# Five edits in the last stages of a four-layer convolution chain on one core: how the largest value is found, filling products, order of the first stacking, banks and split of the last convolution

## The chip, the cores and the metric

The kernel runs on one core of a Trainium2 chip. The metric is the device time of one execution in microseconds (us).

## What is computed

The input has 16 images of 32 channels, 28 by 28. Cut to its core, the reference is:

```
# layer 0: ternary weights, 32 -> 192 -> 192 -> 32 channels, plus the input
h = relu6(bn(conv1x1(x, ternarize(w1))));  h = relu6(bn(conv3x3(h, ternarize(w2))))
x = x + bn(conv1x1(h, ternarize(w3)))
# layer 1: two 3x3 convolutions of values rounded to 8 bits; the step is max(x)/255 over the WHOLE tensor
out = relu(bn(conv3x3(fake_quant_act(x), fake_quant_weight(w1))))
x = relu(bn(conv3x3(fake_quant_act(out), fake_quant_weight(w2))) + x)
# layers 2 and 3 (here "c" and "d"), each:
y = relu(bn(conv3x3(x, w) + b))
x = where(max|y| over the image of a channel < 0.001, 0, y)
```

## The kernel before

The 16 images are four chunks `c` of four images `g` (`NCH = 4`, `G = 4`); a chunk's four images of 32 channels fill the 128 partitions, 784 pixels in the free dimension. Every engine has its own instruction stream, written by hand, and waits on semaphores. The long first part (layer 0, one image after the other in `slot`) is untouched. The work around the change comes after it:

- **Projection of the last chunk.** `project(c, h, steps)` multiplies the output of layer 0's 3x3 convolution by `w3` for half `h` of the rows. Steps 0 and 1 read `h2a` (the first 128 hidden channels, as a high and a low part; semaphore `h2a_ready`), steps 2 and 3 read `h2b` (the other 64; `h2_ready`). Each step is four products of 128x392 into 32 output partitions each. VectorE (DVE) then adds the residual (`residual`, line 1026) and reduces each half to a maximum (line 1029). `keep_warm(n, bank)` (line 370) issues n products into a bank that nobody reads.
- **The global maximum.** `step(k)` on VectorE and `largest(n)` on TensorE (PE) find the largest value over all partitions, once ahead of each 8-bit convolution: a column maximum `mx` (line 1145), a transpose into one row (line 547), a reduction of that row (line 1147), a product with ones that copies the number to all partitions (line 549), the clamp at 1e-8 (line 1149), the reciprocal (line 1150).
- **The 8-bit convolutions.** `qconv` (line 559) is nine taps for each half chunk. VectorE scales (`ra`), ScalarE (ACT) rounds into `qi` (`quant`, line 774). ScalarE also rescales the residual `y0` of each chunk (line 799).
- **The tail.** A written list sets the order on all engines; "q" is the second 8-bit convolution, "c" and "d" are layers 2 and 3:

```
TAIL = [("q", 0), ("q", 1), ("q", 2), ("c", 0), ("q", 3), ("c", 1), ("d", 0), ("c", 2), ("d", 1),
        ("c", 3), ("d", 2), ("d", 3)]
```

For each chunk of "q" VectorE adds the residual into `t1` (in the array `va`, line 1249), and splits it into a high and a low half-precision part (`part`, lines 1253 and 1255). `stack(layer, c)` copies the parts into `kst` (in the array `big`): six pieces of 32x900 on VectorE (line 1224, or 1226 in layer d), two on ScalarE (line 813 or 815). The stacked 64 partitions are doubled to 128, by VectorE itself for four of the eight (layer, chunk) pairs (line 1232, semaphore `v_dup`), by a DMA on SP's queue for the others (line 289, `s_dup`). `lconv(layer, c)` (line 590) is 72 products of 32 columns of weights: two halves of nine taps of four products, one product for each image. `relu_l` (ScalarE, line 827) writes each half into `yb` (in the array `vh`). For "d" VectorE reduces both halves (line 1279), forms the mask `keep` (line 1281), and for the last chunk multiplies both halves by it (line 1285); SP then writes each half out (line 302).

Three waits of `lconv` matter: for the doubled stack, for the weights, and for the bank. Layer c uses PSUM banks 2 and 3, layer d banks 4 and 5 (`bank = 2 + 2 * layer`), so each convolution of a layer waits until ScalarE has read the one before it (`wait(pe, yb_ready, 2 * DONE_BEFORE[...])`).

Of the kernel before, what the change touches and what calls it, by code (L numbers as in the profile page):

```python
# [28 lines left out]
P = 128  # L29
B, C, H, W = 16, 32, 28, 28  # L30
HID = 192
G = P // C
# [47 lines left out]
PBANK = (0, 2, 3, 1)  # L80
QBANK = (0, 6)
LTAIL = [s for s in TAIL if s[0] != "q"]
DONE_BEFORE = {(k, c): (LTAIL.index((k, c - 1)) + 1 if c else 0) for k, c in LTAIL}

N1, N2, N3 = C * HID, HID * HID * TAPS, HID * C


def conv_seq(nc, x, params, w1, w2a, w2b, w3, wq1, wq2, wc, wd, out):
    with ExitStack() as ctx:
# [109 lines left out]
        keep_ready, last_ready = sem("keep_ready"), sem("last_ready")  # L199
# [50 lines left out]
        @block.sync  # L250
        def _(sp):
            for k in range(2):
                dy = slice(3 * HID * k, 3 * HID * k + 3 * HID)
                sp.dma_start(w2ar[:, dy], w2a[:, dy]).then_inc(s_w2a[k], 16)
            sp.dma_start(xin[:, 0, :], x[:, 0, :]).then_inc(s_x[0], 16)
            sp.dma_start(w2ar[:, 6 * HID:], w2a[:, 6 * HID:]).then_inc(s_w2a[2], 16)
            sp.dma_start(w3r[:, 0, :], w3[0:P]).then_inc(s_w3, 16)
            sp.dma_start(w3r[0:HB, 1, :], w3[P:HID]).then_inc(s_w3, 16)
            sp.dma_start(w3r[HB:P, 1, :], w3[P:HID]).then_inc(s_w3, 16)
            sp.dma_start(w2br[HB:P, :], w2b).then_inc(s_w2c, 16)  # L260
            for c in range(1, NCH):
# [12 lines left out]
            for g in range(G):  # L274
                q = slice(C * g, C * g + C)
                for k, w in enumerate((wq1, wq2)):
                    sp.dma_start(wqr[q, k, :], w).then_inc(s_wq, 16)
                for k, w in enumerate((wc, wd)):
                    sp.dma_start(wcr[q, k, :], w).then_inc(s_wc, 16)
            for c in range(1, NCH):  # L280
                spread(c)

            def dup(layer, c):

                if (layer, c) in V_DUP:
                    return
                sp.wait_ge(stack_v[layer], c + 1)
                sp.wait_ge(stack_a[layer], c + 1)
                sp.dma_start(kst[2 * C:P, layer, c % 2].rearrange("p g h w -> p (g h w)"),
                             kst[0:2 * C, layer, c % 2].rearrange("p g h w -> p (g h w)")).then_inc(s_dup[layer][c], 16)  # L290

            for kind, c in TAIL:
                if kind == "q":
                    dup(0, c)
                elif kind == "c":
                    dup(1, c)
                else:
                    pieces = 1 if c < NCH - 1 else 2
                    for h in range(pieces):
                        px = slice(HW // pieces * h, HW // pieces * (h + 1))  # L300
                        sp.wait_ge(*((o_ready, c + 1) if pieces == 1 else (last_ready, h + 1)))
                        sp.dma_start(out[:, c, px], om[:, c, px]).then_inc(s_out, 16)
            sp.wait_ge(s_out, 16 * (NCH + 1))

# [48 lines left out]
        def _(pe):  # L353
# [94 lines left out]
                                             skip_group_check=True)  # L448
                i.then_inc(convb_done, 1)

            def project(c, h, steps=(0, 1, 2, 3), bank=7):

                wait(pe, y0_ready, 2 * c + h if bank == 7 else 0)
                lower = slice(HB * h, HB * h + HB)
                for s in steps:
                    if s < 2:
                        pe.wait_ge((h2a_ready, h2_ready)[s], (c + 1) * G)
                    for g in range(G):
                        w, rhs = ((w3t[:, 0, :], h2a[:, g, s, HALF * h:HALF * h + HALF]) if s < 2 else
                                  (w3t[lower, 1, :], h2b[lower, g, s - 2, :]))  # L460
                        i = nc.tensor.matmul(ps[C * g:C * g + C, bank, :HALF], w, rhs, start=(s == 0), stop=(s == 3))  # L461
                if 3 in steps:
                    i.then_inc(proj_done, 1)
# [71 lines left out]
                slot(NCH - 1, g, last=True)  # L535

            pe.wait_ge(rb_ready, 2 * B)
            keep_warm(16, 6)
            project(NCH - 1, 0, (0,))
            project(NCH - 1, 1, (0,), bank=6)  # L540
            project(NCH - 1, 0, (1, 2, 3))
            project(NCH - 1, 1, (1, 2, 3), bank=6)

            def largest(n):

                pe.wait_ge(gm_go, 2 * n + 1)
# [28 lines left out]
            def lconv(layer, c):  # L575
# [9 lines left out]
                for h in range(2):  # L585
                    for t in range(TAPS):
                        dy, dx = divmod(t, 3)
                        r0 = HALF_ROWS * h + dy
                        for g in range(G):
                            i = nc.tensor.matmul(ps[C * g:C * g + C, bank + h, :HALF],  # L590
                                                 wst[:, layer, C * t:C * t + C],
                                                 kst[:, layer, c % 2, g, r0:r0 + HALF_ROWS, dx:dx + W],
                                                 start=(t == 0), stop=(t == TAPS - 1))
                    i.then_inc(lconv_done[layer], 1)

# [9 lines left out]
        def _(act):  # L605
# [187 lines left out]
                quant(c, 1)  # L793

            act.wait_ge(scale_ready, 2)
            for c in range(NCH):
                if c >= 2:
                    quant(c, 1)
                nc.scalar.activation(y0[:, c, :], y0[:, c, :], ACT.Identity, bias=col[:, SIG + 3:SIG + 4],
                                     scale=col[:, BD + 2:BD + 3]).then_inc(ys_ready, 1)  # L800

            def stack(layer, c):

# [14 lines left out]
            def relu_l(layer, c):  # L818
# [6 lines left out]
                for h in range(2):  # L825
                    act.wait_ge(lconv_done[layer], 2 * c + h + 1)
                    nc.scalar.activation(yb[:, n % 2, HALF * h:HALF * h + HALF], ps[:, 2 + 2 * layer + h, :HALF],  # L827
                                         ACT.Relu, bias=bn[:, BSH, k:k + 1],
                                         scale=col[:, SIG + 4 + layer:SIG + 5 + layer]).then_inc(yb_ready, 1)

            for kind, c in TAIL:
                if kind == "q":
                    stack(0, c)
                else:
                    relu_l("cd".index(kind), c)
                    if kind == "c":
                        stack(1, c)


        @block.vector  # L840
        def _(dve):
# [301 lines left out]
            def step(k):  # L1143
                dve.wait_ge(cmax_done, 2 * NCH * (k + 1))
                red(mx[:, 8:9], cm[:, k].rearrange("p c h -> p (c h)"), AX.X, ALU.max).then_inc(gm_go, 1)
                dve.wait_ge(gm_done, 2 * k + 1)
# [96 lines left out]
            for kind, c in TAIL:  # L1243
# [29 lines left out]
                else:  # L1273
                    at = LTAIL.index((kind, c))
                    m = keep[:, at:at + 1]
                    px = [slice(HALF * h, HALF * h + HALF) for h in range(2)]
# [4 lines left out]
                    ts(m, cm[:, 1, c, 0:1], cm[:, 1, c, 1:2], CUT, ALU.max, ALU.is_ge).then_inc(keep_ready, 1)  # L1281
                    if c == NCH - 1:
                        dve.wait_ge(keep_ready, at + 1)
                        for h in range(2):
                            ts(om[:, c, px[h]], yb[:, at % 2, px[h]], m, None, ALU.mult).then_inc(last_ready, 1)


# [45 lines left out]
```

## Time and profile before

| | us |
|---|---|
| median of 3 executions | 316.2 (316.17 to 317.35) |
| the profiled execution | 316.51 |
| its span, first to last instruction | 314.7 |
| TensorE busy in the span | 269.9 (86%) |
| VectorE busy | 260.5 (83%) |
| ScalarE busy | 183.4 (58%) |
| mean granted clock of TensorE | 0.988 of full speed |

The busy shares are averages over very different stages. From about 224 us on, which this change is about, the engines take turns; there the times at which an instruction starts, and what it waited for, tell more than shares do. All line numbers in rows are those of the kernel before.

### The profile page before, as it was taken

To read this page: it belongs to the slowest core of one execution; us is meant where nothing else is said; L and a number is where in the kernel's file an instruction comes from. 1 tells how busy PE (TensorE), PEld (TensorE's weight loads), DVE (VectorE), ACT (ScalarE), POOL (GpSimd) and SP (SyncE) were. 2 spreads that over 40 slices of the span, in tenths; PEclk is the share of its full clock that TensorE was granted. 3 is DMA by queue.
4 is the path that set the end of the run, shared out by engine and by line. 5 is a ranking of instruction groups with operands and counts; after the bars stand their busy time and mean duration, and the time that the engine had idled before them with its cause. 6 is when DMAs were issued, how large, how long until landed. Compare 5 with 4: busy or idle time off the path is not lost.

```text
span 314.7 us, 6016 instructions
## 1 busy us (share of the span) xinstructions
PE 269.9 (86%) x2341; PEld 149.8 (48%) x2341; DVE 260.5 (83%) x497; ACT 183.4 (58%) x262; POOL 13.1 (4%) x24
## 2 busy tenths in 40 slices
PE   1458898899999999999999999999989997474763
PEld 0223554455555555555555554555545454242432
DVE  6599989999999888898888897857377588999983
ACT  3686775856836756645575666583236393447541
POOL 4500000000000000000000000030000000000101
PEclk9999999999999999999999999999999999899979
DMA  7832002022100000000000000000000000502232
GB/s 213 228 79 53 2 1 72 15 68 53 27 2 0 2 0 3 0 0 0 0 0 0 0 2 1 2 0 2 0 2 0 0 2 1 118 3 61 70 95 102
DMA packets 5656, 10.07 MB, mean 32 GB/s; under 512 B 1729, under 2 KB 3969, under 8 KB 5633
## 3 DMA queue, kind: packets, MB, share of 16 engines
q1 hardware_dynamic: 5360, 9.27, 11.0%
q10 hardware_dynamic: 272, 0.49, 0.7%
q8 instruction: 15, 0.25, 0.3%
q14 instruction: 9, 0.07, 0.1%
HBM read 4.04 MB, written 1.61 MB: 18 GB/s over the span
## 4 chain that ended last, share of the span: by engine, by line
PE 58%; DVE 21%; ACT 8%; issue 6%; DMA 4%; POOL 1%; ACTq 0%; DVEq 0%
PE ps L421 13%; PE ps L417 8%; PE ps L407 8%; PE ps L446 7%; PE ps L442 5%; PE ps L559 4%; PE ps L431 4%; PE ps L384 3%; DMA par<-params_in 3%; DVE big L1226 2%; PE ps L590 2%; DVE va L967 2%; ACT big L813 2%; PE ps L461 2%; DVE vh L973 1%
## 5 line engine op out<-in xcount | busy, mean ns | idle before, releaser
L421 PE MATMUL ps<-hb,w2bt 128*128 128x392 f16 x288 | 55.0, 334 | 0.0
L590 PE MATMUL ps<-big,wst 128*32 128x392 f16 x576 | 28.6, 358 | 17.8 <-ACT vh L827 10.8
L669 ACT CAST vh<-va 128x1680 f16<-128x1680 f32 x16 | 25.5, 1592 | 30.3 <-PE ps L446 25.4
L417 PE MATMUL ps<-vh,w2at 128*128 128x392 f16 x192 | 37.9, 333 | 0.8 <-DVE ps L997 0.8
L421 PEld LDWEIGHTS ps<-hb,w2bt 128*128 128x128 f16 x288 | 27.7, 96 | 21.9
L407 PE MATMUL ps<-vh,wu 128*128 128x392 f16 x192 | 37.1, 345 | 1.0 <-DVE vh L973 1.0
L967 DVE TENSOR_TENSOR va<-hp 128x420 f32<-128x420 f32 x64 | 33.9, 592 | 0.5
L651 ACT ACTIVATE part<-ps,bn 128x392 f32<-128x392 f32 x32 | 21.7, 678 | 16.8 <-PE ps L384 16.7
L973 DVE TENSOR_TENSOR vh<-va,vh 128x1680 f16<-128x1680 f32 x16 | 30.5, 1908 | 0.5
L590 PEld LDWEIGHTS ps<-big,wst 128*32 128x32 f16 x576 | 16.6, 103 | 29.8 <-issue 14.9
L651 ACT ACTIVATE ra<-ps,bn 128x392 f32<-128x392 f32 x32 | 21.6, 676 | 13.6 <-PE ps L384 11.8
L446 PE MATMUL ps<-hb,w2bt 128*64 128x392 f16 x288 | 27.6, 334 | 0.0
L407 PEld LDWEIGHTS ps<-vh,wu 128*128 128x128 f16 x192 | 19.1, 100 | 16.2 <-issue 1.8
L384 PE MATMUL ps<-xk,w1t 96*128 (+1 forms) x60 | 20.6, 344 | 6.6 <-ACT part L651 5.7
L559 PE MATMUL ps<-qi,wqi 128*128 128x392 bf16 x144 | 25.0, 333 | 0.2
L417 PEld LDWEIGHTS ps<-vh,w2at 128*128 128x128 f16 x192 | 18.5, 97 | 14.0 <-DVE ps L997 1.1
L675 ACT ACTIVATE r2a<-ps,bn 128x784 f32<-128x784 f32 x16 | 16.0, 1000 | 12.5 <-DVE h2a L1013 6.0
L446 PEld LDWEIGHTS ps<-hb,w2bt 128*64 128x64 f16 x288 | 16.3, 108 | 8.6
L431 PE MATMUL ps<-vh,wu 128*64 128x392 f16 x96 | 19.4, 340 | 0.0
L431 PE MATMUL ps<-vh,wun 128*64 128x392 f16 x96 | 19.4, 339 | 0.0
L442 PE MATMUL ps<-vh,w2at 128*64 128x392 f16 x192 | 19.3, 337 | 0.0
L559 PEld LDWEIGHTS ps<-qi,wqi 128*128 128x128 bf16 x144 | 13.8, 97 | 11.3 <-ACT qi L774 1.0
(200 smaller groups left out, 409.8 us busy)
## 6 DMA issues: line engine op xcount, KB each, us to landing
xk<-xpart SPq DMA_DIRECT2D x45, 49.0 KB, 1.9
big<-big SPq DMA_DIRECT2D x4, 450.0 KB, 3.8
xin<-x_in SPq DMA_DIRECT2D x4, 392.0 KB, 8.5
y_out<-xin SPq DMA_DIRECT2D x3, 392.0 KB, 2.4
big<-w2a_in SPq DMA_DIRECT2D x3, 288.0 KB, 4.1
big<-w2b_in ACTq DMA_DIRECT2D x1, 432.0 KB, 6.4
big<-w2b_in SPq DMA_DIRECT2D x1, 432.0 KB, 8.2
y_out<-xin SPq DMA_DIRECT2D x2, 196.0 KB, 2.0
```

Of the source, the lines that this page charges most:

```text
L384: nc.tensor.matmul(ps[:, bank, :HALF], (w1t[:, 0:P], w1t[:, P:P + 2 * HB])[two], xk[:, j, HALF * h:HALF * h + HALF], start=True, stop=True ...
L407: i = nc.tensor.matmul(ps[:, PBANK[k], :HALF], weights(k, dx, False), vh[:, b, part, k, :, dx:dx + W], start=(part == 0 and dx == 0), stop ...
L417: nc.tensor.matmul(ps[:, PBANK[k], :HALF], weights(k, dx, False), vh[:, b, part, k, :, dx:dx + W], start=False, stop=False, skip_group_che ...
L421: i = nc.tensor.matmul(ps[:, PBANK[k], :HALF], w2bt[:, t, 0:P], rows(b, k // 3, t), start=False, stop=(t == TAPS - 1), skip_group_check=True)
L431: i = nc.tensor.matmul(ps[HB * q:HB * q + HB, 4, :HALF], weights(k, dx, True), vh[:, b, part, k, :, dx:dx + W], start=(part == 0 and dx == 0),
L442: nc.tensor.matmul(ps[HB * q:HB * q + HB, 5, :HALF], weights(k, dx, True), vh[:, b, part, k, :, dx:dx + W], start=False, stop=False, skip_ ...
L446: i = nc.tensor.matmul(ps[HB * q:HB * q + HB, 5, :HALF], w2bt[:, t, P:HID], rows(b, q, t), start=False, stop=(t == TAPS - 1), skip_group_c ...
L559: i = nc.tensor.matmul(ps[:, bank + h, :HALF], wqi[:, k, t, :], qi[:, c, r0:r0 + HALF_ROWS, dx:dx + W], start=(t == 0), stop=(t == TAPS - 1))
L590: i = nc.tensor.matmul(ps[C * g:C * g + C, bank + h, :HALF], wst[:, layer, C * t:C * t + C], kst[:, layer, c % 2, g, r0:r0 + HALF_ROWS, dx ...
L651: nc.scalar.activation(dst[:, HALF * h:HALF * h + HALF], ps[:, bank, :HALF], ACT.Relu, bias=bn[:, BSH, at:at + 1], scale=bn[:, BSC, at:at ...
L967: i = tt(va[:, k], d[x0], d[x1], op)
L973: tt(vh[:, b, 1].rearrange(v), va[:].rearrange(v), vh[:, b, 0].rearrange(v), ALU.subtract).then_inc(va_ready, 1)
```

## The change

1. **Partition maximum by one product.** `largest` is now one product: the column `mx` is repeated to 128 columns of weights (`mx[:, 8:9].to_broadcast([P, P])`), and the identity streams through, so that every partition receives the row of all 128 maxima. VectorE reduces that 128x128 result directly to a column, and clamps it.
2. **Fewer filling products.** Ahead of the last projection stood 16; now there are 3 ahead of it and 4 in its middle. Steps 0 and 1 of both halves go first and wait only for `h2a_ready`; steps 2 and 3 wait for `h2_ready`.
3. **First stack ahead of later rounding.** On ScalarE `stack(0, 0)` comes before the rounding and the rescaling of chunk 3.
4. **Last convolution in free banks.** ("d", 3) uses banks 0 and 1, and does not wait for `yb_ready`; instead it waits for `t1_ready` of chunk 2.
5. **Uneven halves.** ("d", 3) is split into 18 and 10 rows (504 and 280 pixels) instead of 14 and 14; the last multiplication by `keep` is shared: VectorE the first 392 pixels, ScalarE the last 392, each with a semaphore of its own.

```diff
+LBANK = {(k, c): 2 + 2 * "cd".index(k) for k, c in LTAIL}
+LBANK["d", NCH - 1] = 0
+DONE_BEFORE["d", NCH - 1] = 0
+LROWS = {(k, c): (HALF_ROWS, HALF_ROWS) for k, c in LTAIL}
+LROWS["d", NCH - 1] = (18, 10)
+def row_slices(k, c):
+    first = LROWS[k, c][0]
+    return slice(0, first), slice(first, H)
...
-                        sp.wait_ge(*((o_ready, c + 1) if pieces == 1 else (last_ready, h + 1)))
+                        sp.wait_ge(*((o_ready, c + 1) if pieces == 1 else (last_ready[h], 1)))
...
-                    if s < 2:
-                        pe.wait_ge((h2a_ready, h2_ready)[s], (c + 1) * G)
+                    if s in (0, late):
+                        pe.wait_ge(h2_ready if s else h2a_ready, (c + 1) * G)
...
-            keep_warm(16, 6)
-            project(NCH - 1, 0, (0,))
-            project(NCH - 1, 1, (0,), bank=6)
-            project(NCH - 1, 0, (1, 2, 3))
-            project(NCH - 1, 1, (1, 2, 3), bank=6)
+            keep_warm(3, 4)
+            project(NCH - 1, 0, (0, 1), late=2)
+            project(NCH - 1, 1, (0, 1), bank=6, late=2)
+            keep_warm(4, 4)
+            project(NCH - 1, 0, (2, 3), late=2)
+            project(NCH - 1, 1, (2, 3), bank=6, late=2)
...
-                nc.tensor.transpose(ps[0:1, 5, 0:P], mx[:, 8:9], ident[:]).then_inc(gm_done, 1)
-                pe.wait_ge(gm_go, 2 * n + 2)
-                nc.tensor.matmul(ps[:, 5, 0:1], ones[0:1, :], rowm[0:1, 0:1], start=True,
+                nc.tensor.matmul(ps[:, 5, 0:P], mx[:, 8:9].to_broadcast([P, P]), ident[:], start=True,
                                  stop=True).then_inc(gm_done, 1)
...
-                bank = 2 + 2 * layer
+                bank = LBANK["cd"[layer], c]
                 wait(pe, yb_ready, 2 * DONE_BEFORE["cd"[layer], c])
+                if ("cd"[layer], c) == ("d", NCH - 1):
+                    pe.wait_ge(t1_ready, NCH - 1)
...
             for kind, c in TAIL:
                 if kind == "q":
                     stack(0, c)
+                    if c == 0:
+                        quant(NCH - 1, 1)
+                        shifted(NCH - 1)
...
+            nc.scalar.mul(om[:, NCH - 1, HALF:HW], yb[:, at % 2, HALF:HW], keep[:, at:at + 1]).then_inc(last_ready[1], 1)
...
-                red(rowm[0:1, 0:1], ps[0:1, 5, 0:P], AX.X, ALU.max).then_inc(gm_go, 1)
-                dve.wait_ge(gm_done, 2 * k + 2)
-                link(ts(c1(GM + k), ps[:, 5, 0:1], 1e-8, None, ALU.max))
+                link(red(c1(GM + k), ps[:, 5, 0:P], AX.X, ALU.max))
+                link(ts(c1(GM + k), c1(GM + k), 1e-8, None, ALU.max))
```

The change moves instructions at three places. On TensorE, behind the last product of layer 0 (the `h2a` and `h2b` rows are the projection, w2at rows the fillers, `ident,mx` the maximum), stood:

```order
L370 MATMUL ps<-vh,w2at 128x392 x16
L461 MATMUL ps<-h2a,w3t 32x392 x12
L461 MATMUL ps<-h2b,w3t 32x392 x8
L461 MATMUL ps<-h2a,w3t 32x392 x4
L461 MATMUL ps<-h2b,w3t 32x392 x8
L370 MATMUL ps<-vh,w2at 128x392 x8
L547 MATMUL ps<-ident,mx 1x128
L549 MATMUL ps<-rowm,ones 128x1
```

and there stands now:

```order
L383 MATMUL ps<-vh,w2at 128x392 x3
L474 MATMUL ps<-h2a,w3t 32x392 x16
L383 MATMUL ps<-vh,w2at 128x392 x4
L474 MATMUL ps<-h2b,w3t 32x392 x16
L383 MATMUL ps<-vh,w2at 128x392 x8
L561 MATMUL ps<-ident,mx 128x128
```

All `h2a` products now stand ahead of all `h2b` products, with four fillers between them, and the maximum is one product of 128x128.

On ScalarE, ahead of and in the first stacks (`qi` is the rounding, `y` the rescaling, `big` the stacking), stood:

```order
L799 ACTIVATE y<-y,col 128x784 [waits scale_ready]
L799 ACTIVATE y<-y,col 128x784
L774 ACTIVATE qi<-ra,magic 128x15x28 [waits q_v]
L774 ACTIVATE qi<-ra,magic 128x13x28 [waits q_v]
L799 ACTIVATE y<-y,col 128x784
L774 ACTIVATE qi<-ra,magic 128x15x28 [waits q_v]
L774 ACTIVATE qi<-ra,magic 128x13x28 [waits q_v]
L799 ACTIVATE y<-y,col 128x784
L813 COPY big<-part 32x900 [waits part_ready0]
L813 COPY big<-part 32x900
```

and there stands now:

```order
L811 ACTIVATE y<-y,col 128x784 [waits scale_ready]
L811 ACTIVATE y<-y,col 128x784
L787 ACTIVATE qi<-ra,magic 128x15x28 [waits q_v]
L787 ACTIVATE qi<-ra,magic 128x13x28 [waits q_v]
L811 ACTIVATE y<-y,col 128x784
L830 COPY big<-part 32x900 [waits part_ready0]
L830 COPY big<-part 32x900
L787 ACTIVATE qi<-ra,magic 128x15x28 [waits q_v]
L787 ACTIVATE qi<-ra,magic 128x13x28 [waits q_v]
L811 ACTIVATE y<-y,col 128x784
```

The two stacking copies of chunk 0 moved ahead of three instructions of chunk 3.

On TensorE, the last three convolutions (("c", 3), ("d", 2), ("d", 3)) and their waits were:

```order
L590 MATMUL ps<-big,wst 32x392 [waits yb_ready,s_dup0_3]
L590 MATMUL ps<-big,wst 32x392 x71
L590 MATMUL ps<-big,wst 32x392 [waits yb_ready,s_dup1_2]
L590 MATMUL ps<-big,wst 32x392 x71
L590 MATMUL ps<-big,wst 32x392 [waits yb_ready,v_dup]
L590 MATMUL ps<-big,wst 32x392 x71
```

and are now:

```order
L603 MATMUL ps<-big,wst 32x392 [waits yb_ready,s_dup0_3]
L603 MATMUL ps<-big,wst 32x392 x71
L603 MATMUL ps<-big,wst 32x392 [waits yb_ready,s_dup1_2]
L603 MATMUL ps<-big,wst 32x392 x71
L603 MATMUL ps<-big,wst 32x504 [waits t1_ready,v_dup]
L603 MATMUL ps<-big,wst 32x504 x35
L603 MATMUL ps<-big,wst 32x280 x36
```

The last one has lost its wait for ScalarE's reads of the one before it, and has 36 wider and 36 narrower products.

## Rows read from the trace of the kernel before

**Rows 1.** Timeline from 216 us: start, length, engine, line, what, idle time before

```profile
224.38 2.83 PE L370 MATMUL ps<-vh,w2at 128*128 128x392 f16 x16
...
225.60 0.57 DVE L1019 SCALAR_TENSOR_TENSOR h2b<-r2b,h2b 128x392 f16<-128x392 f32 x1
227.13 0.68 PE L461 MATMUL ps<-h2a,w3t 128*32 128x392 f16 x12
...
227.75 0.51 PE L461 MATMUL ps<-h2b,w3t 64*32 64x392 f16 x8
...
228.31 0.62 DVE L1026 SCALAR_TENSOR_TENSOR y<-ps,bn,xin 128x392 f32<-128x392 f32 x1 [2.15 <-PE ps L461]
```

**Rows 2.** The same timeline, at the first global maximum

```profile
231.14 0.27 PE L547 MATMUL ps<-ident,mx 128*1 128x128 f32 x1 [0.72 <-DVE mx L1145]
231.45 0.28 DVE L1147 TENSOR_REDUCE rowm<-ps 1x1 f32<-1x128 f32 x1 [0.45 <-PE ps L547]
...
231.78 0.38 PE L549 MATMUL ps<-rowm,ones 1*128 1x1 f32 x2 [0.37 <-DVE rowm L1147]
...
232.19 0.16 DVE L1149 TENSOR_SCALAR col<-ps 128x1 f32<-128x1 f32 x1 [0.47 <-PE ps L549]
232.39 0.16 DVE L1150 RECIPROCAL col<-col 128x1 f32<-128x1 f32 x1
```

**Rows 3.** Timeline from 256 us, at the first stacks

```profile
255.79 4.40 PE L559 MATMUL ps<-qi,wqi 128*128 128x392 bf16 x25
255.79 0.98 DVE L1255 SCALAR_TENSOR_TENSOR part<-va,part 128x784 f16<-128x784 f32 x1
...
256.81 1.12 ACT L774 ACTIVATE qi<-ra,magic 128x420 bf16<-128x420 f32 x2
256.81 2.38 DVE L1224 COPY big<-part 32x900 f16<-32x900 f16 x6
257.83 1.03 ACT L799 ACTIVATE y<-y,col 128x784 f32<-128x784 f32 x1
258.77 1.88 ACT L813 COPY big<-part 32x900 f16<-32x900 f16 x2
260.74 1.09 DVE L1232 COPY big<-big 64x3600 f16<-64x3600 f16 x1 [1.55 <-ACT big L813]
...
261.98 3.24 PE L590 MATMUL ps<-big,wst 128*32 128x392 f16 x72 [1.79 <-DVE big L1232]
...
264.56 1.90 ACT L813 COPY big<-part 32x900 f16<-32x900 f16 x2 [3.92 <-DVE part L1255]
...
265.16 3.23 PE L559 MATMUL ps<-qi,wqi 128*128 128x392 bf16 x18
```

**Rows 4.** Chain of work that ended last, 296 to 315: start, length, what

```profile
305.73 0.69 ACT vh L827
...
306.55 3.27 PE ps L590 x70
...
309.84 0.69 ACT vh L827
...
310.55 0.57 DVE cm L1279
```

**Rows 5.** Timeline of the end

```profile
301.20 4.47 PE L590 MATMUL ps<-big,wst 128*32 128x392 f16 x72 [4.09 <-DMA big<-big]
...
303.99 1.09 DVE L1232 COPY big<-big 64x3600 f16<-64x3600 f16 x1
...
311.40 0.76 DVE L1285 TENSOR_SCALAR xin<-vh,keep 128x392 f32<-128x392 f32 x2
311.85 0.81 SPq L302 DMA_DIRECT2D y_out<-xin  x2
```

**Rows 6.** Busy time by stretch; third column from the end: PEclk

```profile
226.00:228.00 2.00, 2.00 (x28) 0.84 (x25) 0.17 (x1) 0.00 (x0) 0.00 (x0) 1.00 0.00 0
...
300.00:302.00 2.00, 0.80 (x12) 0.44 (x16) 1.85 (x4) 0.82 (x1) 0.00 (x0) 0.60 0.77 258
```

More of the change, by code:

```diff
@@ L198, in conv_seq @@
         v_dup = sem("v_dup")
-        keep_ready, last_ready = sem("keep_ready"), sem("last_ready")
+        keep_ready, last_ready = sem("keep_ready"), [sem(f"last_ready{h}") for h in range(2)]
         part_ready = [sem(f"part_ready{l}") for l in range(2)]
@@ L449, in pair_outer, with project @@
                 i.then_inc(convb_done, 1)
-            def project(c, h, steps=(0, 1, 2, 3), bank=7):
+            def project(c, h, steps=(0, 1, 2, 3), bank=7, late=1):
                 wait(pe, y0_ready, 2 * c + h if bank == 7 else 0)
@@ L537, in _ @@
             pe.wait_ge(rb_ready, 2 * B)
-            keep_warm(16, 6)
-            project(NCH - 1, 0, (0,))
-            project(NCH - 1, 1, (0,), bank=6)
-            project(NCH - 1, 0, (1, 2, 3))
-            project(NCH - 1, 1, (1, 2, 3), bank=6)
+            keep_warm(3, 4)
[4 more added lines that the diff above has]
+            project(NCH - 1, 1, (2, 3), bank=6, late=2)
             def largest(n):
-                pe.wait_ge(gm_go, 2 * n + 1)
-                nc.tensor.transpose(ps[0:1, 5, 0:P], mx[:, 8:9], ident[:]).then_inc(gm_done, 1)
-                pe.wait_ge(gm_go, 2 * n + 2)
-                nc.tensor.matmul(ps[:, 5, 0:1], ones[0:1, :], rowm[0:1, 0:1], start=True,
+                pe.wait_ge(gm_go, n + 1)
+                nc.tensor.matmul(ps[:, 5, 0:P], mx[:, 8:9].to_broadcast([P, P]), ident[:], start=True,
                                  stop=True).then_inc(gm_done, 1)
@@ L582, in lconv @@
                     pe.wait_ge(s_dup[layer][c], 16)
-                bank = 2 + 2 * layer
+                bank = LBANK["cd"[layer], c]
                 wait(pe, yb_ready, 2 * DONE_BEFORE["cd"[layer], c])
-                for h in range(2):
+                if ("cd"[layer], c) == ("d", NCH - 1):
+                    pe.wait_ge(t1_ready, NCH - 1)
+                for h, rows in enumerate(row_slices("cd"[layer], c)):
                     for t in range(TAPS):
                         dy, dx = divmod(t, 3)
-                        r0 = HALF_ROWS * h + dy
                         for g in range(G):
-                            i = nc.tensor.matmul(ps[C * g:C * g + C, bank + h, :HALF],
+                            i = nc.tensor.matmul(ps[C * g:C * g + C, bank + h, :W * (rows.stop - rows.start)],
                                                  wst[:, layer, C * t:C * t + C],
-                                                 kst[:, layer, c % 2, g, r0:r0 + HALF_ROWS, dx:dx + W],
+                                                 kst[:, layer, c % 2, g, dy + rows.start:dy + rows.stop, dx:dx + W],
                                                  start=(t == 0), stop=(t == TAPS - 1))
@@ L795, in _, with shifted @@
             act.wait_ge(scale_ready, 2)
-            for c in range(NCH):
-                if c >= 2:
-                    quant(c, 1)
+            def shifted(c):
                 nc.scalar.activation(y0[:, c, :], y0[:, c, :], ACT.Identity, bias=col[:, SIG + 3:SIG + 4],
                                      scale=col[:, BD + 2:BD + 3]).then_inc(ys_ready, 1)
+            for c in range(NCH - 1):
+                if c == 2:
+                    quant(c, 1)
+                shifted(c)
             def stack(layer, c):
@@ L824, in relu_l @@
                     act.wait_ge(*((part_ready[1], 2 * c2 + 2) if k2 == "c" else (o_ready, c2 + 1)))
-                for h in range(2):
+                for h, rows in enumerate(row_slices("cd"[layer], c)):
+                    px = slice(W * rows.start, W * rows.stop)
                     act.wait_ge(lconv_done[layer], 2 * c + h + 1)
-                    nc.scalar.activation(yb[:, n % 2, HALF * h:HALF * h + HALF], ps[:, 2 + 2 * layer + h, :HALF],
+                    nc.scalar.activation(yb[:, n % 2, px], ps[:, LBANK["cd"[layer], c] + h, :px.stop - px.start],
                                          ACT.Relu, bias=bn[:, BSH, k:k + 1],
@@ L837, in _ @@
                         stack(1, c)
+            at = LTAIL.index(("d", NCH - 1))
+            act.wait_ge(keep_ready, at + 1)
+            nc.scalar.mul(om[:, NCH - 1, HALF:HW], yb[:, at % 2, HALF:HW], keep[:, at:at + 1]).then_inc(last_ready[1], 1)
         @block.vector
@@ L1145, in step @@
                 red(mx[:, 8:9], cm[:, k].rearrange("p c h -> p (c h)"), AX.X, ALU.max).then_inc(gm_go, 1)
-                dve.wait_ge(gm_done, 2 * k + 1)
-                red(rowm[0:1, 0:1], ps[0:1, 5, 0:P], AX.X, ALU.max).then_inc(gm_go, 1)
-                dve.wait_ge(gm_done, 2 * k + 2)
-                link(ts(c1(GM + k), ps[:, 5, 0:1], 1e-8, None, ALU.max))
+                dve.wait_ge(gm_done, k + 1)
+                link(red(c1(GM + k), ps[:, 5, 0:P], AX.X, ALU.max))
+                link(ts(c1(GM + k), c1(GM + k), 1e-8, None, ALU.max))
                 link(nc.vector.reciprocal(c1(RS + k), c1(GM + k)))
@@ L1275, in _ @@
                     m = keep[:, at:at + 1]
-                    px = [slice(HALF * h, HALF * h + HALF) for h in range(2)]
+                    px = [slice(W * rows.start, W * rows.stop) for rows in row_slices(kind, c)]
                     for h in range(2):
@@ L1283, in _ @@
                         dve.wait_ge(keep_ready, at + 1)
-                        for h in range(2):
-                            ts(om[:, c, px[h]], yb[:, at % 2, px[h]], m, None, ALU.mult).then_inc(last_ready, 1)
+                        ts(om[:, c, 0:HALF], yb[:, at % 2, 0:HALF], m, None, ALU.mult).then_inc(last_ready[0], 1)
 def kernel(**inputs):
```

## The prediction, made before the changed kernel ran

> **What bounds the kernel now.** I read the chain that ended last first, then the timeline around each edit. From 224 us on no engine is the bound by itself; the chain hops between them, and what counts at each edit is which wait ends last.
>
> At 224.38 TensorE has finished layer 0, issues 16 fillers and reaches the first projection product only at 227.13; VectorE, whose residual needs both halves of the projection input, has had its last input (`h2b`) ready at 225.60 + 0.57 = 226.17 and then idles 2.15 us until 228.31 [rows 1]. The fillers are therefore on the path. Then comes the row of small steps of the global maximum: 231.14, 231.45, 231.78, 232.19, 232.39, each waiting for the one before [rows 2]; it occurs twice. At the first stack VectorE is ready at 256.81 + 2.38 = 259.19, but its doubling copy starts at 260.74, for ScalarE's two pieces ran from 258.77 only [rows 3]. From there to the last stack VectorE's own work sets the time, so a start that is earlier there moves everything behind it. At the end the last convolution starts at 306.55, behind ScalarE's read of the bank (305.73 + 0.69), and is followed by a read of 0.69 and a reduction of 0.57 [rows 4].
>
> **Edit 2, fewer fillers.** A filler takes (227.13 − 224.38) / 16 = 0.172 us. Three take 0.52: the `h2a` products start at 224.90. Three groups of four `h2a` products and the change of step behind them took 227.75 − 227.13 = 0.62, or 0.21 a group; the four groups now take 0.83, to 225.73. Four fillers, 0.69, to 226.42; with 0.1 for the change of tile, the `h2b` products start at about 226.5 instead of 227.75 [rows 1]. The gain is **1.25 us**. It can't exceed 227.75 − 226.2 = 1.55, since `h2b` isn't there before; with 0.2 us at each of three changes between fillers and products instead of 0.1 in all it would be 0.75. The eight fillers behind the projection and the maximum move with it, so no idle time of TensorE grows here. The granted clock is 1.00 in this stretch, that is 2.4 GHz [rows 6].
>
> **Edit 1, the maximum.** Before, from the transpose to the reciprocal: 232.39 − 231.14 = 1.25 us. Now: the product (M), the reduction of 128 columns (0.28 and 0.03 to the next; it read 128 elements of a partition before too) and a clamp (0.20, as between 232.19 and 232.39) [rows 2]. The gain is 1.25 − 0.51 − M = 0.74 − M. A product of this shape in single precision with 128 weight columns and 128 streaming columns isn't in the trace. Nearest rows: the product with ones is two passes with 128 weight columns and one streaming column, 232.19 − 231.78 = 0.41 to its reader; the transpose streams 128 columns once in 0.27, while 392 half-precision columns take 0.172 of issue, so 128 single-precision ones cost some 0.1. Two such streams, the first partly hidden behind the second weight load, make M = 0.41 + 0.10 to 0.20. I take 0.56: **0.18 us a time, 0.36 for both**. Bounds: M = 0.46 (one stream exposed by half) gives +0.28 a time, M = 0.85 (four streams exposed) gives −0.11.
>
> The rows show one record for the transpose and two for the product with ones [rows 2], and so two streams at least. A rule of the Trainium skill speaks against the edit: "TensorE: Matmul & The Clock Gate", section Terms, has transpose mode as four times faster for FP32 than an ordinary product. By that rule there are four streams, M is 0.41 + 0.3 = 0.71, and both steps together gain 0.06 us instead of 0.36; no run here yet shows which.
>
> The ten fillers behind the maximum (1.7 us) still fit ahead of the first rounded data. VectorE's order and waits stay, and TensorE waits once less.
>
> **Edit 3, the first stack.** ScalarE's three instructions of chunk 3 (256.81 to 258.86) now come behind its stack. The stack needs VectorE's parts, ready at 255.79 + 0.98 = 256.77, and can start at about 256.9 when the rescaling of chunk 2 has ended; it ends at 258.8, ahead of VectorE's own six pieces at 259.19. The doubling starts at 259.25 instead of 260.74: **1.49 us**. TensorE has its last product of chunk 2 at 260.19, so the convolution that waits for the doubling (261.98) can start at 260.5: little more than that was to be had [rows 3]. Cover for what is moved back: chunk 3's rounding, now ready at about 260.0, is first read by the products at 265.16 − 1.49 = 263.7 [rows 3]; its rescaled residual is read by VectorE only behind layer c's first stack. Both engines copying pieces at once costs nothing new: ScalarE's two took 1.90 at 264.56 beside VectorE's, and 1.88 at 258.77 mostly alone [rows 3]. If ScalarE's next stack (263.06 now) had to wait for chunk 3's work, it would lose; that ends at 260.9, 2.1 us ahead. Bounds 1.3 and 1.55.
>
> **Edit 4, free banks.** The doubled stack for the last convolution is ready at 303.99 + 1.09 = 305.08 [rows 5]. Convolution ("d", 2) ends at 301.20 + 4.47 = 305.67 [rows 5]; its last group of four started some 0.35 before and another can follow after 3.24 / 18 = 0.18 [rows 3], at 305.50. The last convolution now starts there and not at 306.55 [rows 4]: **1.05 us**. If a switch costs a full drain it starts at 305.70: 0.85. Convolution ("d", 2) took 4.47 here and 3.24 elsewhere [rows 3, 5], because the clock granted behind its 4.09 us wait was low (0.60 on average from 300 to 302 [rows 6], the lower level being 1.2 GHz); in an execution in which it is not, the new order can begin only at 305.1 (`v_dup`), which is 0.36 more, not 1.2. So 0.85 to 1.41.
>
> **Edit 5, uneven halves.** If time goes by columns, both halves together cost as before. ScalarE's read: 784 elements 1.03 [rows 3], 392 elements 0.69 [rows 4], so 280 elements 0.59: 0.10 less. VectorE's reduction: 0.57 for 392 [rows 4] and 0.28 for 128 [rows 2], so 280 take 0.45: 0.12 less. The first half's longer read and reduction (0.79 and 0.69, begun 1.0 us ahead of the second's products' end) stay hidden. The shared multiplication gains **nothing**: SP issues the two writes one after the other, 0.81 for both [rows 5], and the second can't be issued before about 0.4 behind the first whoever multiplies; ScalarE's piece would be ready at 0.65 behind `keep`, the write is issued at 0.85. Together **0.22 us**. Bound below: if four narrow products cost as much as four of 392 columns (0.18), the second half is 0.42 longer, and the edit loses 0.2.
>
> **The sum.** 1.25 + 0.36 + 1.49 + 1.05 + 0.22 = 4.37 us. From the profiled execution, 316.51 − 4.37 = 312.14 (its span 310.3 of 314.7). The median before is 0.31 lower, of three runs that spread over 1.2 us; I forecast **312.0 us**.
>
> **Rivals.**
> - *Four streams* (0.12). The product streams its 128 columns not twice but four times, three of them exposed: M = 0.41 + 0.3 = 0.71, 312.0 + 2 × 0.15 = 312.3. For it: single precision already costs 0.1 for 128 columns in one record, twice the half-precision rate. Against it: only two records. This is where the rule of the Trainium skill on transpose mode (above) would lead.
> - *A dear product* (0.05). The repeated column as weights or four passes make M over 0.9: the maximum loses 0.2 or more each time, 312.0 + 0.36 + 0.4 = 312.8. For it: no such form in the trace; against it: the product with ones takes 0.19 a record [rows 2].
> - *The narrow half isn't faster* (0.08). Issue, not columns, sets four narrow products: 312.0 + 0.42 = 312.4. For it: four products take 0.18 where one full one takes 0.172, so each start costs something. Against it: that is only 0.003 for each.
> - *The clock falls once more* (0.06). With 15 instead of 24 fillers a fall in the projection or the first 8-bit convolution doubles a product (0.172 to 0.33); ("d", 2) shows that a fall costs about 1.2 to 1.6 us: 313.6. Against it: TensorE was busy without a break here and still is.
> - *The start gained at the first stack is lost again* (0.04), because a DMA doubling or a rounding comes last further on: 313.5. Against it: the next read of what was moved is 3.7 us later.
> - *Slower than before* (0.02). One mechanism: the clock falls at the thinner projection and stays at 1.2 GHz through the 8-bit convolutions. Each product then costs 0.16 more; 28 products cancel the gain of 4.37, 38 make it slower by over 0.5%, all 144 give 335. Against it: the one low stretch here ended within 4 us of dense products.
>
> **How the numbers follow.** The forecast's own case has 0.63 and 311.0 to 312.9. The bounds of all edits together give a gain between 0.75 − 0.22 + 1.3 + 0.85 − 0.2 = 2.5 and 1.55 + 0.56 + 1.55 + 1.41 + 0.22 = 5.3, that is 311.2 to 314.0; it is unlikely that all lie at one end. With the offset of single runs I give **310.9 to 313.6**. A difference under 0.5% (1.6 us) can't be told from none: faster 0.95, same 0.03, slower 0.02.
>
> **What would show it.** In the changed profile: VectorE's first residual about 1.25 earlier and its wait well under 1 us; reciprocal 1.07 behind the start of the product (1.25 before); doubling copy of chunk 0 right behind VectorE's sixth piece, with no wait for ScalarE; the last two convolutions without a gap; the last reduction about 0.45 long; the two writes still 0.4 apart. The prediction is wrong if a PEclk under 1.00 appears between 224 and 260 us, if the product takes over 0.9 us to its reader, or if a wait of over 0.5 us appears that wasn't there.

## The result

The changed kernel takes **311.62 us** (median of 4 executions, 311.14 to 312.2) against 316.49 (316.17 to 317.35) before; the ratio is 0.9843, with a 95% interval of 0.9816 to 0.9870. The forecast was 312.0. In a later group of runs the ratio was 0.9866 (0.9842 to 0.9891), median 312.36.

The profiled execution took 312.2 us, with a span of 310.4 us and a mean clock of 0.970. Its timeline at the projection answers to [rows 1]:

```profile
223.46 0.67 PE L383 MATMUL ps<-vh,w2at 128*128 128x392 f16 x3
...
224.06 0.85 PE L474 MATMUL ps<-h2a,w3t 128*32 128x392 f16 x16
...
224.68 0.57 DVE L1043 SCALAR_TENSOR_TENSOR h2b<-r2b,h2b 128x392 f16<-128x392 f32 x1
...
224.84 0.84 PE L383 MATMUL ps<-vh,w2at 128*128 128x392 f16 x4
...
225.61 0.54 PE L474 MATMUL ps<-h2b,w3t 64*32 64x392 f16 x16
...
226.18 0.63 DVE L1050 SCALAR_TENSOR_TENSOR y<-ps,bn,xin 128x392 f32<-128x392 f32 x1 [0.93 <-PE ps L474]
```

From the first filler to VectorE's first residual 2.72 us pass, where it was 228.31 − 224.38 = 3.93; VectorE's idle time ahead of it fell from 2.15 to 0.93. TensorE's wait ahead of the maximum grew instead, from 0.72 to 1.43 (first row below); VectorE's chain sets the time there, and the granted clock stayed at 1.00. The same timeline at the first maximum, for [rows 2]:

```profile
229.01 0.46 PE L561 MATMUL ps<-ident,mx 128*128 128x128 f32 x2 [1.43 <-DVE mx L1169]
...
229.50 0.29 DVE L1171 TENSOR_REDUCE col<-ps 128x1 f32<-128x128 f32 x1 [0.64 <-PE ps L561]
229.83 0.15 DVE L1172 TENSOR_SCALAR col<-col 128x1 f32<-128x1 f32 x1
230.02 0.16 DVE L1173 RECIPROCAL col<-col 128x1 f32<-128x1 f32 x1
```

The product has two records and reaches its reader in 0.49 us (0.53 the second time); product to reciprocal is 1.01 and 1.04 where it was 1.25 twice. At the first stack, for [rows 3]:

```profile
254.23 1.89 ACT L830 COPY big<-part 32x900 f16<-32x900 f16 x2
254.23 2.38 DVE L1247 COPY big<-part 32x900 f16<-32x900 f16 x6
256.15 1.14 ACT L787 ACTIVATE qi<-ra,magic 128x420 bf16<-128x420 f32 x2
256.64 1.09 DVE L1255 COPY big<-big 64x3600 f16<-64x3600 f16 x1
```

Both engines copy side by side, and the doubling copy starts 0.03 us behind VectorE's pieces instead of 1.55. The end, for [rows 4, 5], in the chain and (two lines) the timeline:

```profile
293.21 3.84 DMA big<-big
297.06 0.04 issue
297.10 8.60 PE ps L603 x138
...
305.73 0.59 ACT vh L845
...
306.35 0.46 DVE cm L1302
...
307.07 0.62 ACT xin L861
```

```profile
307.07 0.42 DVE L1307 TENSOR_SCALAR xin<-vh,keep 128x392 f32<-128x392 f32 x1
307.53 0.33 SPq L315 DMA_DIRECT2D y_out<-xin  x1
```

The pause between the last two convolutions is gone, yet from the first product of ("d", 2) to the end of the last one of ("d", 3) the time is 8.57 us, and it was 8.59 (301.20 to 309.79). The windows of the same run show why:

```profile
294.00:296.00 2.00, 0.00 (x0) 0.00 (x0) 1.93 (x7) 0.93 (x2) 0.92 (x1) 0.76 0.85 180
296.00:298.00 2.00, 0.90 (x12) 0.46 (x16) 1.85 (x4) 0.92 (x1) 0.00 (x0) 0.50 0.74 251
298.00:300.00 2.00, 2.00 (x28) 0.97 (x24) 1.91 (x6) 1.17 (x2) 0.00 (x0) 0.50 0.04 8
300.00:302.00 2.00, 2.00 (x32) 1.04 (x28) 1.55 (x2) 0.69 (x1) 0.00 (x0) 0.53 0.00 0
302.00:304.00 2.00, 2.00 (x48) 1.01 (x44) 0.59 (x2) 0.68 (x1) 0.00 (x0) 1.00 0.00 0
```

The third column from the end is the granted clock. It was 0.50 (1.2 GHz) up to about 302, under some 4.8 us of dense products; before, under some 2.6 us of them (301.2 to 303.8).

The span's difference, 314.7 − 310.4 = 4.3, is then: projection 1.21, maximum 0.24 + 0.21, first stack 1.52, last two convolutions 0.02, end 0.18, and **0.92 that no edit brought**: the first filler stands at 223.46 instead of 224.38. That comes from the loading: GpSimd begins the batch-norm scales when the parameters' DMA has landed, at 8.39 instead of 9.87, and VectorE's wait for them ended at 13.04 instead of 13.97:

```profile
13.04 0.23 DVE L934 TENSOR_SCALAR bn<-bn,col 128x2 f32<-128x2 f32 x1 [2.22 <-POOL bn L351]
```

The instructions up to the first filler are those of before, and in the twelve other profiles of this study, one of the old code among them (13.09), this line stands between 12.94 and 13.78, with a middle of 13.2. So most of the 0.92 is the late start of the profiled execution before (13.97, later than all others, by 0.8 against their middle); the changed kernel's 13.04 is 0.2 early. At its end about 1.0 of what edit 4 was to bring is missing.

### The profile page after: what moved, and what is told of

Its sections match the earlier page's. It is cut to its first block, busy times and chain, and to the rows that moved or that the text cites. A ratio compares the mean times of both kernels' runs of the same rounds, so it can differ in the third digit from the quotient of the medians.

```text
span 310.4 us, 5994 instructions
## 1 busy us (share of the span) xinstructions
PE 270.6 (87%) x2330; PEld 150.0 (48%) x2330; DVE 260.2 (84%) x496; ACT 184.2 (59%) x263; POOL 13.6 (4%) x24
## 4 chain that ended last, share of the span: by engine, by line
PE 60%; DVE 22%; issue 6%; ACT 5%; DMA 3%; POOL 1%; ACTq 0%; DVEq 0%
PE ps L434 13%; PE ps L430 9%; PE ps L420 9%; PE ps L459 7%; PE ps L455 5%; PE ps L571 5%; PE ps L444 4%; PE ps L397 3%; PE ps L603 3%; DVE big L1249 3%; DVE va L991 2%; DMA par<-params_in 2%; PE ps L474 2%; DVE big L1247 1%; DVE va L1272 1%
## 5 line engine op out<-in xcount | busy, mean ns | idle before, releaser
L603 PE MATMUL ps<-big,wst 128*32 128x392 f16 (+2 forms) x576 | 32.2, 391 | 12.7 <-ACT vh L845 8.3
L603 PEld LDWEIGHTS ps<-big,wst 128*32 128x32 f16 x576 | 18.2, 111 | 26.8 <-issue 12.5
```

What stands on the lines that cost most here:

```text
L603: i = nc.tensor.matmul(ps[C * g:C * g + C, bank + h, :W * (rows.stop - rows.start)], wst[:, layer, C * t:C * t + C], kst[:, layer, c % 2, ...
```

## The experiments

Theory 1: each edit is worth what its own place shows, and edit 4's gain was hidden in that one execution by a longer low clock. Theory 2: the products into the free banks are slow by themselves. Each kernel was profiled; since executions differ by up to 1 us at the start, and in the clock, places are compared from one event to the next, in us. Columns: first filler to first residual; maximum to reciprocal (first, second); VectorE's wait ahead of the doubling copy; first product of ("d", 2) to the end of ("d", 3); from there to the end of the span; median and ratio to the kernel before, measured beside it.

| kernel | residual | maximum | wait | d2+d3 | end | median | ratio (95%) |
|---|---|---|---|---|---|---|---|
| before | 3.93 | 1.25, 1.25 | 1.55 | 8.59 | 4.91 | 316.49 | |
| changed | 2.72 | 1.01, 1.04 | 0.03 | 8.57 | 4.73 | 311.62 | 0.9843 (0.9816 to 0.9870) |
| changed again | 2.71 | 1.00, 1.04 | 0.04 | 7.94 | 4.71 | 312.36 | 0.9866 (0.9842 to 0.9891) |
| 4 undone | 2.71 | 1.01, 1.04 | 0.04 | 8.99 | 4.66 | 312.90 | 0.9885 (0.9861 to 0.9908) |
| fillers | 2.71 | 1.01, 1.04 | 0.04 | 6.66 | 4.64 | 311.60 | 0.9850 (0.9825 to 0.9876) |
| fillers, 4 undone | 2.71 | 1.01, 1.04 | 0.04 | 7.37 | 4.71 | 311.60 | 0.9861 (0.9831 to 0.9891) |
| 1 undone | 2.72 | 1.25, 1.25 | 0.03 | 7.68 | 4.75 | 312.36 | 0.9885 (0.9851 to 0.9919) |
| 2 undone | 3.94 | 1.01, 1.04 | 0.03 | 7.94 | 4.69 | 313.29 | 0.9915 (0.9882 to 0.9947) |
| 3 undone | 2.71 | 1.01, 1.04 | 1.56 | 7.93 | 4.66 | 313.52 | 0.9913 (0.9888 to 0.9939) |
| 5 undone | 2.72 | 1.01, 1.04 | 0.03 | 7.80 | 4.95 | 312.61 | 0.9889 (0.9863 to 0.9916) |
| ScalarE writes | 2.72 | 1.01, 1.03 | 0.04 | 7.94 | 4.67 | 311.76 | 0.9854 (0.9830 to 0.9877) |
| VectorE multiplies | 2.72 | 1.01, 1.04 | 0.03 | 7.86 | 4.68 | 311.73 | 0.9855 (0.9831 to 0.9879) |
| all together | 2.50 | 1.01, 1.04 | 0.04 | 7.17 | 4.75 | 310.96 | 0.9829 (0.9810 to 0.9849) |
| before, with fillers | 3.93 | 1.24, 1.25 | 1.56 | 7.36 | 4.87 | 314.39 | 0.9946 (0.9927 to 0.9965) |

The end column spreads over 0.11 us among kernels with the same end (4.64 to 4.75), so it can't carry differences of 0.05. Two distances inside it are steadier: from the start of ScalarE's last read to the start of the mask `keep` 1.09 or 1.10 with uneven halves, 1.30 or 1.31 with even ones; and from the start of the mask to the end of the span 3.53 to 3.55 in all fourteen profiles.

**The changed kernel again.** 

> The changed kernel once more, beside the others of this group. Theory 1 (the gain of the free banks was swallowed by a longer low clock in the profiled execution, which differs from one execution to the next): the time from the first product of the convolution (d, 2) to the last product of (d, 3) is between 7.6 and 8.7 us and follows the length of the low stretch in its own profile; median 311.1 to 312.1. Theory 2 (products into banks 0 and 1 beside ScalarE's reads are slow by themselves): 8.6 us whatever the clock.

```profile
297.85 7.94 PE L603 MATMUL ps<-big,wst 128*32 128x392 f16 x144 [4.11 <-DMA big<-big]
```

7.94, not 8.57: here the clock was 1.00 up to 298 and again from 302 on, so fewer of the products ran at the low level. That is theory 1, and against theory 2, which had 8.6 whatever the clock. The median, 312.36, lies just above the expected 311.1 to 312.1.

**Edit 4 undone.**

```diff
-LBANK["d", NCH - 1] = 0
-DONE_BEFORE["d", NCH - 1] = 0
-                if ("cd"[layer], c) == ("d", NCH - 1):
-                    pe.wait_ge(t1_ready, NCH - 1)
```

> Edit 4 undone alone: (d, 3) back in banks 4 and 5 with the wait for ScalarE's reads; the 18 and 10 rows stay. Theory 1: a pause of 0.9 us of TensorE between (d, 2) and (d, 3) is back; from the first product of (d, 2) to the last of (d, 3) its (d, 2) plus 4.15 us (8.6 if (d, 2) takes 4.5, 9.7 if it takes 5.6); median 0.4 to 1.1 us above the changed kernel, 312.0 to 312.7. Theory 2: no difference, 311.6.

Its timeline has the pause again:

```profile
297.85 4.87 PE L599 MATMUL ps<-big,wst 128*32 128x392 f16 x72 [4.12 <-DMA big<-big]
303.60 3.24 PE L599 MATMUL ps<-big,wst 128*32 128x504 f16 x72 [0.87 <-ACT vh L841]
```

This pair is the cleanest of the study. Here and in the changed kernel run beside it ScalarE's second read of ("d", 2) starts at the same 302.78, so ("d", 2) cost the same in both; the last products end 8.99 and 7.94 behind the first. **Edit 4 is worth 1.05 us at that clock**, and theory 2 falls. The medians, 312.90 and 312.36, differ by 0.54, and their ranges overlap.

**Fillers in the tail's waits**, into bank 0:

```diff
+            FILL = {("c", 1): 22, ("c", 2): 11, ("d", 2): 20}
...
+                n = FILL.get(("cd"[layer], c), 0)
+                if n:
+                    pe.wait_ge(t1_ready, NCH - 1)
+                for _ in range(n):
+                    nc.tensor.matmul(ps[:, 0, :HALF], w2at[:, 0, 0:P], hb[:, 0, 0:HALF_ROWS, 0:W],
+                                     start=True, stop=True)
```

> The changed kernel with filling products in three of the tail's waits of TensorE (22 ahead of (c, 1), 11 ahead of (c, 2), 20 ahead of (d, 2)), into bank 0. Theory 1: the granted clock stays at 1.00 from 230 us on; (d, 2) takes 3.24 us and not 4.5 to 5.6; (d, 3) begins when its doubled stack is there, 3.9 us behind the start of (d, 2), so the last product ends 7.3 us behind it and not 8.6; median 310.4 (310.0 to 310.9). Theory 2: still 8.6 us, 311.6. A third: the fillers themselves delay the convolutions behind them, over 312.

```profile
292.91 3.49 PE L595 MATMUL ps<-hb,w2at 128*128 128x392 f16 x20
297.60 3.24 PE L611 MATMUL ps<-big,wst 128*32 128x392 f16 x72 [1.20 <-DMA big<-big]
301.02 3.24 PE L611 MATMUL ps<-big,wst 128*32 128x504 f16 x72 [0.18 <-DVE big L1263]
```

("d", 2) takes 3.24 us and ("d", 3) now waits for the doubled stack, as theory 1 has it. The DMA ahead of ("d", 2) took 4.4 us to land here and 3.8 to 3.9 elsewhere, which shortens the 6.66 by half a microsecond and lengthens what stands ahead of it. The expectation missed twice: between 274 and 282 us the clock still fell (0.75 and 0.82 on average), behind the 2.74 us wait ahead of ("d", 0) that got no fillers, and the median is 311.60 (310.74 to 312.35) where 310.4 was expected. Against the changed kernel's 312.36 beside it the gain is 0.8, but single executions overlap (310.74 to 312.35 against 311.63 to 312.88).

**The same with edit 4 undone.** 

> The same fillers with edit 4 undone. Theory 1: with the clock at 1.00 the free banks are worth only 0.1 to 0.2 us, since the doubled stack comes 3.9 us behind the start of (d, 2), and ScalarE's read ends 4.0 behind it: 310.6, that is 0.1 to 0.2 above the run with fillers and free banks. If the free banks were worth their 1.05 us at every clock, 311.4.

7.37; the run with fillers, free banks and a DMA of usual length (all together, below) has 7.17. At full clock the free banks are worth 0.20, not 1.05. The medians, both 311.60, can't resolve that, and lie 1.0 above the expected 310.6.

**Edits 1, 2, 3 and 5 undone**, one at a time, each by its lines in the diff above (for 5 also the shared multiplication).

> Edit 1 undone alone: transpose, reduction of one row, product with ones. My sum: from the first product of the maximum to the reciprocal 1.25 us instead of 1.01 and 1.04, twice; 0.45 us slower than the changed kernel, 312.1. The rival (four streams make the new product as long as the two old ones): no difference.

> Edit 2 undone alone: 16 fillers ahead of the projection, old order. My sum: VectorE's first residual starts 3.93 us behind the first filler instead of 2.72; 1.2 us slower, 312.8. If the missing fillers were what lengthens the low clock of the tail, the old fillers would bring the low stretches back to 3.4 us each and the time would stay at about 311.8.

> Edit 3 undone alone: ScalarE rounds and rescales chunk 3 ahead of the first stack. My sum: the doubling copy starts 1.5 us later behind VectorE's sixth piece, and everything behind it; 1.5 us slower, 313.1. The rival (the start is lost again further on): under 0.5 us slower.

> Edit 5 undone alone: halves of 14 and 14 rows, and both last multiplications on VectorE; free banks stay. My sum: last read 0.68 instead of 0.58, last reduction 0.56 instead of 0.45, the two writes issued as before; from the last product's end to the end of the span 4.88 instead of 4.70; 0.2 us slower, 311.8. If the narrow half costs as much as a half of 392 columns, then this one is faster by 0.2.

By their places: edit 1 is worth 0.24 + 0.21 = 0.45 us, edit 2 1.23, edit 3 1.53, edit 5 0.21 (1.31 against 1.10 from the last read to the mask; 0.24 by the coarser end column). Nothing gained at one place was lost at another: from the reciprocal of the second maximum to the first doubling copy all kernels with edit 3 have 9.99 to 10.00 us, without it 11.52, and from there to ("d", 2) 40.44 to 40.49 (but 40.98 where the DMA was late). That second distance holds through a low clock in between as well: in the changed kernel ("c", 1) and ("d", 0) took 9.22 us together, more than half of it at 1.2 GHz, in the run with all together (below) 3.24 each, and the distance is 40.46 in both. The changed kernel wasn't run beside these four. By their ratios the medians of edits 2 and 3 (313.29 and 313.52) lie above both of its groups (their intervals just touch that of the second); those of 1 and 5 (312.36 and 312.61, expected 312.1 and 311.8) are too coarse to show 0.45 and 0.21. The rival in the second expectation fell as well: with 16 fillers the low clock was there too (0.50 from 299 to 302).

**The last write from ScalarE's queue.**

```diff
+            act.wait_ge(last_ready[1], 1)
+            act.dma_start(out[:, NCH - 1, HALF:HW], om[:, NCH - 1, HALF:HW]).then_inc(s_out, 16)
```

> The changed kernel with the last write issued from ScalarE's own queue, right behind its multiplication, not from SP's behind the first write. My step (SP's issue of two writes in turn is what hides the shared multiplication): the last write is issued 0.2 us earlier (at 0.65 behind keep instead of 0.85), end of the span behind the last product 4.5 instead of 4.71. Rival (the end is set by something else in the writes): 4.71. A time 0.2 us lower can't be told from none by the medians; the profile decides.

```profile
306.74 0.62 ACT L863 ACTIVATE xin<-vh,keep 128x392 f32<-128x392 f32 x1 [0.76 <-DVE keep L1308]
...
307.39 0.37 ACTq L865 DMA_DIRECT2D y_out<-xin  x1
```

The write was issued 0.69 behind the mask, earlier than SP's second one (0.87), but the span ended 4.67 behind the last product, not 4.5, and 3.55 behind the start of the mask, as everywhere. My expectation was wrong, and the landings say where. The first write was issued 0.49 behind the mask in both kernels and took 1.9 us. The second landed 0.54 behind the first, from ScalarE's queue (2.25 us after its issue) as from SP's (2.06), and in all fourteen profiles the span ends 0.40 behind that landing. So here the end follows the landings, and the issue of the second write had 0.18 us to spare; bringing the first one forward wasn't tried.

**Both last multiplications on VectorE**, uneven halves kept. 

> Uneven halves kept, both last multiplications on VectorE as before the change. My step (the shared multiplication gains nothing, SP issues the second write 0.4 us behind the first whoever multiplies): end of the span behind the last product 4.70 to 4.75, as in the changed kernel (4.71 to 4.73). Rival (the sharing brought half of edit 5's gain): 4.85.

4.68, and 3.54 from the mask to the end, as with the shared multiplication (3.53 and 3.54): sharing gains nothing. Edit 5's 0.21 is all in the shorter last read and reduction.

**All together.** Fillers in five waits (`{("c", 1): 22, ("d", 0): 12, ("c", 2): 11, ("d", 1): 6, ("d", 2): 18}`), two instead of four in the projection, ScalarE's write. 

> All together: the changed kernel, fillers in the tail's waits (22 ahead of (c, 1), 12 ahead of (d, 0), 11 ahead of (c, 2), 6 ahead of (d, 1), 18 ahead of (d, 2)), only two fillers in the middle of the projection, and the last write from ScalarE's queue. Expected: first residual 2.45 behind the first filler (2.72), clock 1.00 to the end, last product 7.2 us behind the first of (d, 2) less what a late DMA takes, 4.5 behind it the end; against the changed kernel 0.3 + 0.5 to 1.3 + 0.2 = 1.0 to 1.8 us, about 310.7. Rival (fillers delay the convolutions behind them more than the clock gives back): 312 or more.

```profile
296.00:298.00 2.00, 1.22 (x32) 0.78 (x36) 1.83 (x5) 1.23 (x2) 0.00 (x0) 1.00 0.50 201
298.00:300.00 2.00, 2.00 (x48) 1.02 (x40) 1.92 (x5) 1.54 (x2) 0.00 (x0) 1.00 0.00 0
```

The clock stays at 1.00 from 256 us on, the residual comes at 2.50, the last two convolutions take 7.17. The median is 310.96 (310.47 to 311.25), the lowest of all, 0.8 below the two variants of the changed kernel run beside it (311.76 and 311.73), with no overlap; 1.0 to 1.8 were expected against the changed kernel, 0.2 of them for the write, which brought nothing. The places say where the gain is: the residual (0.21) and the last two convolutions. Between the first doubling copy and ("d", 2) it is still 40.46 us, so the fillers ahead of ("c", 1), ("d", 0), ("c", 2) and ("d", 1) neither cost nor brought time there. Whether those ahead of ("d", 2) would do alone wasn't run.

**The kernel before, with the first set of fillers.** 

> The kernel before the change with the same fillers as the first run with fillers (22 ahead of (c, 1), 11 ahead of (c, 2), 20 ahead of (d, 2)). Theory 1 (the price of the low clock behind the wait for the DMA is there in the old kernel too, at about 1.2 us): from the first product of (d, 2) to the last of (d, 3) 7.4 us instead of 8.59 in the profile of before, median about 315.2 against 316.4. If the low stretch were a new cost that the changed kernel brought, the fillers would gain nothing here: 8.6 us, 316.4.

7.36 as expected: the low clock cost the old kernel 1.23 us there too, and isn't brought by the change. The median is 314.39, 1.7 us under before beside it (316.10) and under the expected 315.2. That is more than the 1.23 of that one place; the profile of before had a mean clock of 0.988, at the top of what its executions show (0.968 to 0.988, mostly 0.974 to 0.980), so the low stretches of the others may well be longer, which no profile shows.

## Why the prediction was right, and by how much

The mechanism was right for each gain in the sum at the clock of the profile it was read from. Wrong were the upper bound of edit 4, a reason given for edit 5, and two side remarks (below). Step by step, what was forecast and what the places show, in us:

| step | forecast | shown |
|---|---|---|
| edit 2, fewer fillers | 1.25 (0.75 to 1.55) | 1.21; 1.23 undone |
| edit 1, both maxima | 0.36 (−0.22 to 0.56) | 0.45 |
| edit 3, first stack | 1.49 (1.3 to 1.55) | 1.52; 1.53 undone |
| edit 4, free banks | 1.05 (0.85 to 1.41) | 1.05 at an equal low clock, 0.20 at full clock |
| edit 5, uneven halves | 0.22 | 0.21; 0.21 undone |
| shared multiplication | nothing | nothing (3.54 without, 3.53 and 3.54 with, from mask to end) |
| sum | 4.37 | 4.44 |

The sum of what was shown takes 1.21 + 0.45 + 1.52 + 1.05 + 0.21, with edit 4 at the low clock. The measured ratios, times the 316.5 of before, are 5.0 and 4.2 us, on both sides of it.

- **Edit 1.** I took 0.56 us for a form that the trace didn't have; it is 0.49 and 0.53. The rival with four streams (0.71) and the dear product fell. The Trainium skill's rule in "TensorE: Matmul & The Clock Gate", Terms, that transpose mode is four times faster for FP32, doesn't show as a price of that size here: the whole new product needed 0.18 and 0.22 us more to its reader than the transpose did (0.31), and the part with ones that went away had needed 0.41. How much of these times is streaming, the trace doesn't say.
- **Edit 2.** "No idle time of TensorE grows here" was wrong: its wait ahead of the first maximum went from 0.72 to 1.43 us, and one of 0.52 appeared ahead of the first rounded data. Neither cost time, since VectorE's chain sets the pace and the clock stayed at 1.00.
- **Edit 5.** The rival of the narrow half fell: ScalarE's two reads of ("d", 3) start 305.73 − 304.69 = 1.04 us apart, and 309.84 − 308.37 = 1.47 apart before. Nine groups of 280 columns took 0.71 of nine of 392, as their columns are (280 / 392 = 0.71). (That rival's price was 9 × (0.18 − 0.129) = 0.46, not 0.42.) The reason given for the shared multiplication, SP's issue of two writes in turn, isn't what holds the end: with the second write issued earlier the end stayed where it was.
- **Edit 4.** The prediction named the low clock behind the wait for the DMA, and that an execution without it would gain 0.36 more than the sum: 8.59 − 1.05 − 0.36 = 7.18; all together has 7.17. But it counted that 0.36 as part of edit 4's worth ("So 0.85 to 1.41"), measured against a kernel before at its low clock. At full clock the old order is faster too, 7.36, and the edit is worth 0.20, far under the lower bound of 0.85. What it also did not reckon with is the other side. The low stretch can also be longer than in the one profile of before, and in the profile of the changed kernel it took the 1.05 back. In its own terms, "301.20 + 4.47" was taken as a length, while it is one draw: ("d", 2) to ("d", 3) took 7.68 to 8.57 in the eight profiles of kernels with free banks and no fillers there. The low stretch of [rows 6] wasn't "the one low stretch" of before either: ("c", 1), behind a wait of 4.66 us, took 4.87 instead of 3.24.
- **What would show it** named a PEclk under 1.00 between 224 and 260 us, and a wait of over 0.5 that wasn't there. The clock was 1.00. The wait ahead of the first maximum was there but grew by 0.71, and the new one of 0.52 is just over the mark; as both are harmless, this sign was drawn too widely. Of the clock in the tail, where the spread of the time lies, the prediction asked nothing.

That the forecast lay within 0.4 us of the median owes something to chance. The sum was taken from one profiled execution whose start was late by 0.8 and whose clock was at the top of its kernel's range. The first makes an execution longer and the second shorter, and 316.51 came out close to the median. The forecast left only 0.14 for such things, between 312.14 and 312.0.

## What to carry to other kernels

Where engines take turns, price an edit from the event that releases its place to the event that leaves it, and compare profiles there: here those distances repeated to 0.02 us while whole executions differed by over 1 us. (The one that ends at TensorE's last product spread over 0.11.) A serial stretch behind a long wait of TensorE has no fixed length, since the clock granted in it differs from one execution to the next; either keep the engine busy through the wait, or give the edit a price at each of the two clocks. Fillers that stand in front of useful work cost what they take; those inside a wait that was there anyway cost nothing here (40.46 us from the first doubling copy to ("d", 2), with and without them). And a low clock only costs where TensorE's products are what the next step waits for: here in the last two convolutions, not in those before.

## What the hardware showed that I had not expected

- The same wait of 4.1 us ahead of ("d", 2) was followed by 2.6 us of dense products at 1.2 GHz in one execution and by 4.8 us in another; in the changed kernel's profile the clock fell too behind a wait of 2.72 us, where the kernel before had kept 1.00 behind the same wait. In the run with all together, where the longest wait left to TensorE in the tail was 1.47 us, it stayed at 1.00.
- Issuing the last of two writes 0.18 us earlier, from another queue, didn't move its landing: 0.54 us behind the first write's in all fourteen profiles, with the end of the span 0.40 behind it.
- The same 450 KB copy within the chip took 3.8 to 3.9 us to land in 55 of 56 cases, and 4.4 once.
